# Node stages of a graph kernel: products in groups of four blocks, batch statistics, normalising block by block on ScalarE

## The reference, cut to what matters

```python
h = jnp.maximum(_layernorm(x, axis=-1), 0.0)
x = x + _L0_gnn_ref(h, ...)   # h @ W_w + W_b, attention by edge, weighted segment sum
h = jnp.maximum(_layernorm(x, axis=-1), 0.0)
x = x + _L1_gnn_ref(h, ...)   # a second layer norm inside; edge network; silu(x + agg) @ theta_w + theta_b
h = jnp.maximum(_layernorm(x, axis=-1), 0.0)
x = x + _L2_gnn_ref(h, ...)   # out = relu(x @ Wl + bl + mean_of_neighbours @ Wr + br); out / norm
h = jnp.maximum(_layernorm(x, axis=-1), 0.0)
x = x + _L3_gnn_ref(h, ...)   # h @ W.T, four attention heads, softmax by destination
```

## Time and profile before

| | us |
|---|---|
| median of three runs | 14312.43 (14309.55 to 14322.54) |
| profiled execution, span from first to last instruction | 14155.8 |
| what the runs' median has beyond this span | 156.6 |
| busy: TensorE / VectorE / ScalarE / GpSimd | 6866.6 / 6687.7 / 1674.0 / 7418.7 |

### The profile page before, as it was taken

One profiled execution on the slowest core, in us unless ns is written; L12 is line 12 of the kernel. 1 busy time (PEld: TensorE's weight loads), 2 busy tenths in 40 slices (PEclk: granted clock), 3 DMA queues, 4 the chain that ended last, 5 costly groups with the idle time before them and its releaser, 6 DMA issues. The chain is left out here.

```text
span 14155.8 us, 143364 instructions
## 1 busy us (share of the span) xinstructions
PE 6866.6 (49%) x36068; PEld 6019.9 (43%) x36069; DVE 6687.7 (47%) x23089; ACT 1674.0 (12%) x3503; POOL 7418.7 (52%) x7813
## 2 busy tenths in 40 slices
PE   1013333333344437777777523333233577777776
PEld 0013333333344325555555422222222476767775
DVE  4962222222477775555555432222224455555555
ACT  0001111111222211111111100000000100000000
POOL 0016666666555536666666346666662355555553
PEclk9996666666666668888888755555555555555555
DMA  0214443444333324444444511111113222323225
GB/s 17 105 46 127 128 129 124 129 128 127 115 92 87 91 73 121 120 123 121 121 124 120 109 40 47 47 47 47 47 47 28 58 81 81 81 81 81 81 80 80
DMA packets 1209149, 1249.60 MB, mean 88 GB/s; under 512 B 265607, under 2 KB 992220, under 8 KB 1208880
## 3 DMA queue, kind: packets, MB, share of 16 engines
q0 software_dynamic: 248832, 577.29, 16.5%
q1 hardware_dynamic: 957020, 668.72, 16.4%
q10 hardware_dynamic: 3156, 2.29, 0.0%
HBM read 842.78 MB, written 404.91 MB: 88 GB/s over the span
## 5 line engine op out<-in xcount | busy, mean ns | idle before, releaser
L920 POOL DMA_INDIRECT buf<-node_rows,buf x3456 | 3315.1, 959 | 2330.2 <-issue 1662.0
L1362 POOL DMA_INDIRECT buf<-node_rows_ln,buf x1728 | 1720.8, 996 | 1097.0 <-DVE buf L1491 614.8
L616 POOL DMA_INDIRECT edge_rows_by_src<-buf x1728 | 1686.0, 976 | 1069.3 <-ACT buf L626 547.6
L934 PE MATMUL psum<-buf 128*128 128x129 f32 x3456 | 768.5, 368 | 1796.6 <-issue 1335.2
L663 PE MATMUL psum<-buf 128*128 x3456 | 713.9, 373 | 1712.4 <-ACT buf L635 1155.2
L934 PEld LDWEIGHTS psum<-buf 128*128 128x128 f32 x3456 | 675.9, 276 | 1889.2 <-issue 1503.0
L663 PEld LDWEIGHTS psum<-buf 128*128 128x128 f32 x3456 | 644.7, 278 | 1769.0 <-issue 1768.1
L2024 PE MATMUL psum<-buf 128*128 128x132 f32 x3456 | 874.4, 412 | 576.3 <-issue 567.8
L944 DVE TENSOR_TENSOR agg<-agg,psum 128x129 f32 x864 | 250.4, 290 | 1868.4 <-remote 1609.3
L2024 PEld LDWEIGHTS psum<-buf 128*128 128x128 f32 x3456 | 772.6, 312 | 657.4 <-issue 656.0
L1014 POOL TENSOR_SCALAR buf<-buf 128x128 f32<-128x128 f32 x880 | 690.7, 800 | 665.0 <-PE psum L1064 623.8
(11 more groups left out here) (325 smaller groups left out, 12253.8 us busy)
## 6 DMA issues: line engine op xcount, KB each, us to landing
buf<-edge_rows_by_src SPq DMA_DIRECT2D x114, 1056.0 KB, 7.5
buf<-edge_rows_by_src SPq DMA_DIRECT2D x110, 1024.0 KB
buf<-in_edge_attr SPq DMA_DIRECT2D x864, 128.0 KB
running_weighted_sums<-buf SPq DMA_DIRECT2D x108, 544.0 KB
buf<-loc_rows_by_src SPq DMA_DIRECT2D x110, 512.0 KB
buf<-loc_rows_by_dst SPq DMA_DIRECT2D x110, 512.0 KB
running_sums<-buf SPq DMA_DIRECT2D x108, 512.0 KB
buf<-node_rows,buf POOLq DMA_INDIRECT x3456
```

Source lines behind the costliest of these rows:

```text
L616: nc.gpsimd.indirect_dma_start(rows, bass.IndirectOffsetOnAxis(ap=at[:, h, t:t + 1], axis=0), st[:, h, t, :], None).then_inc(scattered[h], 16)
L920: nc.gpsimd.indirect_dma_start(rows[:, t, 0:used], None, table, bass.IndirectOffsetOnAxis(ap=stage[:, t:t + 1], axis=0)).then_inc(sem, 16)
L934: last = nc.tensor.matmul(ps[:, q // 3, (q % 3) * W:(q % 3) * W + width], oh[:, 2 * q + s, :], rows[:, 2 * q + s, 0:width], start=(s == 0) ...
L1362: nc.gpsimd.indirect_dma_start(xn[:, j, t, :], None, table1, bass.IndirectOffsetOnAxis(ap=stage[:, j // 4, at:at + 1], axis=0)).then_inc(g ...
```

## The change

The helpers of the product are replaced. `GROUPS` are twelve groups of four blocks and one of a single block. `product_tensor` and `product_vector` are unrolled over the groups; `psT`, `hT` and `psO` exist twice and hold four blocks each; TensorE turns group g and then multiplies group g - 1, and VectorE copies group g and then takes out group g - 1. `ln_stats` becomes one batch-statistics instruction for each block and a short combination (`stats_done`). Normalising goes block by block to ScalarE in an activation with scale and offset by partition, also in `l1_nodes` and `l2_nodes`, where VectorE did it. `l1_nodes` splits every later step by groups, and ScalarE's location copies stand behind its second normalising. In `l1_finish` the bias is added before the wait for the sums. In `l2_nodes` the store is cut into four. In `l2_finish` ScalarE's copies are gone, since TensorE reads the table directly; the multiplication by the degree is cut into groups and stands behind the wait for the weights. `l3_nodes` changes as `l0_nodes` does. The edge stages are not touched.

The diff, cut: of the removed lines most are left out, since they stand in the functions printed above.

```diff
+GB = 4
+GROUPS = [(first, min(GB, NB - first)) for first in range(0, NB, GB)]
...
+        self.n = 0
+def stats_of_block(nc, st, b, block):
+    return nc.vector.bn_stats(st.parts[:, b, :], block)
+def stats_done(nc, dve, ch, st):
+    part = lambda k: st.parts[:, :, k:k + 1].rearrange("p b o -> p (b o)")
+    ch.link(nc.vector.tensor_tensor(st.gap[:], part(1), part(4), ALU.subtract))
+    nc.vector.tensor_tensor(st.mean[:], part(1), part(4), ALU.add)
+    ch.link(nc.vector.tensor_tensor(st.var[:], part(2), part(5), ALU.add))
+    ch.link(nc.vector.scalar_tensor_tensor(st.gap[:], st.gap[:], 0.25, st.gap[:], ALU.mult, ALU.mult))
+    ch.link(nc.vector.scalar_tensor_tensor(st.var[:], st.var[:], 1.0 / D, st.gap[:], ALU.mult, ALU.add))
+    nc.vector.tensor_scalar(st.var[:], st.var[:], LN_EPS, None, ALU.add).then_inc(st.var_ready, 1)
+    st.n += 1
+    dve.wait_ge(st.sd_ready, st.n)
+    ch.link(nc.vector.reciprocal(st.rstd[:], st.sd[:]))
+    ch.link(nc.vector.scalar_tensor_tensor(st.nmr[:], st.mean[:], -0.5, st.rstd[:], ALU.mult, ALU.mult))
...
+class NodeProduct:
+    def __init__(self, es, nc, sb, sem, terms):
+        self.terms = terms
+        self.hT = sb([P, 2, terms, GB * P])
+        self.psT = es.enter_context(nc.psum_tensor(fresh("psum"), [P, 2, terms, 512], F32))
+        self.psO = es.enter_context(nc.psum_tensor(fresh("psum"), [P, 2, 512], F32))
+        self.transposed, self.turned, self.produced, self.consumed = (sem() for _ in range(4))
+def product_tensor(nc, pe, m, ident, ready, blocks, weights):
+    for g in range(len(GROUPS) + 1):
+        if g < len(GROUPS):
+            first, count = GROUPS[g]
+            ready(g)
+            if g >= 2:
+                pe.wait_ge(m.turned, g - 1)
+            for k in range(m.terms):
+                for t in range(count):
+                    last = nc.tensor.transpose(m.psT[:, g % 2, k, t * P:(t + 1) * P], blocks(k, g, first + t, t), ident[:])
+            last.then_inc(m.transposed, 1)
+        if g:
+            count, b = GROUPS[g - 1][1], (g - 1) % 2
+            pe.wait_ge(m.turned, g)
+            if g >= 3:
+                pe.wait_ge(m.consumed, g - 2)
+            for t in range(count):
+                for k in range(m.terms):
+                    last = nc.tensor.matmul(m.psO[:, b, t * P:(t + 1) * P], m.hT[:, b, k, t * P:(t + 1) * P], weights[k], start=(k == 0), stop=(k == m.terms - 1))
+            last.then_inc(m.produced, 1)
+def product_vector(nc, dve, m, use):
+    for g in range(len(GROUPS) + 1):
+        if g < len(GROUPS):
+            count = GROUPS[g][1]
+            dve.wait_ge(m.transposed, g + 1)
+            if g >= 2:
+                dve.wait_ge(m.produced, g - 1)
+            nc.vector.tensor_copy(m.hT[:, g % 2, :, 0:count * P], m.psT[:, g % 2, :, 0:count * P]).then_inc(m.turned, 1)
+        if g:
+            first, count = GROUPS[g - 1]
+            dve.wait_ge(m.produced, g)
+            use(g - 1, first, count, m.psO[:, (g - 1) % 2, 0:count * P].rearrange("p (b d) -> p b d", d=D)).then_inc(m.consumed, 1)
...
 def l0_nodes(nc, c, ins, a_src):
...
+                for g, (first, count) in enumerate(GROUPS):
+                    if g >= 2:
+                        act.wait_ge(m.transposed, g - 1)
+                    for t in range(count):
+                        b = first + t
+                        last = nc.scalar.activation(h[:, g % 2, t, :], c["x"][:, b, :], ACT.Relu, bias=st.nmr[:, b:b + 1], scale=st.rstd[:, b:b + 1])
...
+                product_tensor(nc, pe, m, c["ident"], lambda g: pe.wait_ge(staged, g + 1), lambda k, g, b, t: h[:, g % 2, t, :], [w[:]])
...
+                for b in range(NB - 1):
+                    stats_of_block(nc, st, b, c["x"][:, b, :])
+                ch.link(stats_of_block(nc, st, NB - 1, c["x"][:, NB - 1, :]))
+                stats_done(nc, dve, ch, st)
                 dve.sem_inc(stats, 1)
-                ch.link(nc.vector.memset(tab[:], 0.0))
+                nc.vector.memset(tab[:, :, D:W], 0.0)
...
+                product_vector(nc, dve, m, lambda g, first, count, ps: nc.vector.tensor_tensor(
+                    tab[:, first:first + count, 0:D], ps, bc(wb[:].unsqueeze(1), [P, count, D]), ALU.add))
...
 def l1_nodes(nc, c, ins, blk_rows, table1, tab3, keep, loc_by_src):
...
             def _(act):
+                ln_sqrt(nc, act, own, 1)
+                act.wait_ge(own_done, 1)
+                for first, count in GROUPS:
+                    for b in range(first, first + count):
+                        last = nc.scalar.activation(f[:, b, :], c["x"][:, b, :], ACT.Relu, bias=own.nmr[:, b:b + 1], scale=own.rstd[:, b:b + 1])
+                    last.then_inc(rectified, 1)
+                ln_sqrt(nc, act, again, 1)
+                act.wait_ge(again_done, 1)
+                for first, count in GROUPS:
+                    for b in range(first, first + count):
+                        last = nc.scalar.activation(f[:, b, :], f[:, b, :], ACT.Identity, bias=again.nmr[:, b:b + 1], scale=again.rstd[:, b:b + 1])
+                    last.then_inc(normed, 1)
                 for g in range(QC):
                     act.wait_ge(loc_turned, g + 1)
                     nc.scalar.copy(loc_row[:, g].rearrange("p s k -> p (s k)"), psL[:, g % 2, 0:2 * P]).then_inc(loc_kept, 1)
+                for first, count in GROUPS:
+                    act.wait_ge(tabled, first // GB + 1)
+                    nc.scalar.copy(tab3[:, first:first + count, 0, :], f[:, first:first + count]).then_inc(high, 1)
+                for first, count in GROUPS:
+                    act.wait_ge(low_left, first // GB + 1)
+                    nc.scalar.copy(tab3[:, first:first + count, 1, :], tmp[:, first:first + count]).then_inc(middle, 1)
             @block.vector
             def _(dve):
                 ch = Chain(dve, dve_chain)
+                for b in range(NB - 1):
+                    stats_of_block(nc, own, b, c["x"][:, b, :])
+                ch.link(stats_of_block(nc, own, NB - 1, c["x"][:, NB - 1, :]))
+                stats_done(nc, dve, ch, own)
+                dve.sem_inc(own_done, 1)
                 dve.wait_ge(blocks_in, 16)
                 nc.vector.memset(keep[:, 0:1], 0.0)
                 nc.vector.tensor_tensor(keep[:, 1:NPX], pair_blk[:, 1:NPX], pair_blk[:, 0:NPX - 1], ALU.is_equal)
+                for g, (first, count) in enumerate(GROUPS):
+                    dve.wait_ge(rectified, g + 1)
+                    for b in range(first, first + count):
+                        last = stats_of_block(nc, again, b, f[:, b, :])
+                ch.link(last)
+                stats_done(nc, dve, ch, again)
+                dve.sem_inc(again_done, 1)
+                dve.wait_ge(loaded, 32)
+                for g, (first, count) in enumerate(GROUPS):
+                    part = f[:, first:first + count]
+                    dve.wait_ge(normed, g + 1)
+                    ch.link(nc.vector.tensor_tensor(part, part, bc(gb[:, 0:1], [P, count, D]), ALU.mult))
+                    nc.vector.tensor_tensor(part, part, bc(gb[:, 1:2], [P, count, D]), ALU.add).then_inc(tabled, 1)
+                for g, (first, count) in enumerate(GROUPS):
+                    dve.wait_ge(high, g + 1)
+                    nc.vector.tensor_tensor(tmp[:, first:first + count], f[:, first:first + count], tab3[:, first:first + count, 0, :], ALU.subtract).then_inc(low_left, 1)
+                for g, (first, count) in enumerate(GROUPS):
+                    dve.wait_ge(middle, g + 1)
+                    nc.vector.tensor_tensor(tab3[:, first:first + count, 2, :], tmp[:, first:first + count], tab3[:, first:first + count, 1, :], ALU.subtract)
...
 def l1_finish(nc, c, ins, table1, running, last_pairs):
...
+                for g, (first, count) in enumerate(GROUPS):
+                    act.wait_ge(summed, g + 1)
+                    if g >= 2:
+                        act.wait_ge(m.transposed, g - 1)
+                    nc.scalar.activation(h[:, g % 2, 0:count, :], tab[:, first:first + count, 0:D], ACT.Silu).then_inc(staged, 1)
...
+                dve.wait_ge(biased, 16)
+                nc.vector.tensor_tensor(x[:], x[:], bc(b[:].unsqueeze(1), [P, NB, D]), ALU.add).then_inc(based, 1)
+                dve.wait_ge(loaded, 32 + 16 * NB)
+                for first, count in GROUPS:
+                    nc.vector.tensor_tensor(tab[:, first:first + count, 0:D], tab[:, first:first + count, 0:D], agg[:, first:first + count, 0:D], ALU.add).then_inc(summed, 1)
+                dve.wait_ge(based, 1)
+                product_vector(nc, dve, m, lambda g, first, count, ps: nc.vector.tensor_tensor(
+                    x[:, first:first + count, :], x[:, first:first + count, :], ps, ALU.add))
...
 def l2_nodes(nc, c):
...
+                sp.wait_ge(filled, 1)
+                for first in range(0, NB, KB * 2):
+                    end = min(first + KB * 2, NB)
+                    sp.wait_ge(rectified, end)
```

(63 more changed lines are left out.)

122 lines of the change are left out of this document (28 added, 94 removed).

## The result

The changed kernel takes 13954.23 us (median of four runs, 13937.38 to 13969.52) against 14316.62 (four runs, 14309.55 to 14322.54): ratio 0.9743, interval 0.9731 to 0.9755. The forecast was 13980, in a range of 13935 to 14065.

What follows compares the result with a forecast made beforehand. Six node stages, each alone between barriers, were held bound by whole-tensor statistics chains and block-by-block hand-overs. Savings of 70.4, 47, 59, 22, 69 and 64.6 us made 332, taken from 14312.4: 13980 us, range 13935 to 14065.

Steps and rivals of the forecast that it cites:

- The base: Whole kernel: 156.6 us around the 14155.8 us profiled span stay as they are; savings come off the median 14312.43 us.
- Batch statistics: Statistics of the node stages: 0.26 us per instruction (0.20 to 0.43), 14.9 us a set, 13.4 us saved each time.
- Rival 2: Statistics: each batch-statistics instruction costs 0.43 us, giving 14015 us in total; chance 0.10.
- ScalarE's normalising: Node stages: one normalising instruction every 0.386 us, 18.9 us for 49 blocks; lower end 0.25 us.
- The clock: Product stages: TensorE slow for some 5 us, then at 2.4 GHz, a pass falling from 0.215 to 0.107 us.
- rival 1: Product stages: TensorE's clock stays at 1.2 GHz, so only 270 us are saved, 14042 us in total; chance 0.22.
- Product stages: First node stage, l1_finish, l2_finish and last node stage: 24, 30, 43 and 24 us from first feed to last use.
- l1_nodes: This stage: 77.5 us from its start to the last subtraction instead of 125.0, saving 47 us.
- l2_nodes: This stage: 38 us instead of 60.1, saving 22 us, with the last of four stores ending it.
- l2_finish: This stage: saves 69 us, with VectorE idle 3 to 4 us at the start, waiting for the weight loads.
- Rival 3: Product stages: engines don't overlap across groups, 4.3 us a group, 131 us less saved, 14111 us in total; chance 0.05.
- Rival 4: Edge stages: POOL-paced gathers get slower; at 0.08 us more per gather the total is 14395 us; chance 0.03.

## Why the prediction was right, and its terms

The sum was right in its mechanism and 20 us short (332 against 352.0); the total, 13980 against 13954.23, is 0.2% off. Every stage beat its forecast, so no stage's error hid another's; the batch-statistics price is the term that was mis-sized most.

- **The base.** The prediction took the span as 156.6 us short of a timed run for a constant reason. The reason was wrong (above), the step right, and here that was luck: it subtracted from the timed median. Subtracted from the profiled execution's time, the same 332 would have given about 13827.
- **Batch statistics.** Forecast pitch 0.26, bounds 0.20 to 0.43. Measured: (9.57 - 0.28)/48 = 0.194 us, the cheap row's price. A set ends 3.2 us earlier than forecast (12.1 where 14.9 and a hand-over of 0.4 stood); on the path four times, 12.8 of the missing 20 us. Rival 2 is out. The row to go by was that of the 0.20 us instruction; the per-element time of the old reductions misled.
- **ScalarE's normalising** was 0.386 forecast and measured: 18.95 us for 49.
- **The clock** rose 4 to 5 us into the products of every product stage, as forecast from the earlier trace rows; rival 1 (14042 us) is out. The Trainium skill's "TensorE: Matmul & The Clock Gate", Part 4 (PE-mode transpose), has it that the higher clock does not engage for transposes; this case's trace disagrees: 56 transposes with no product among them raised it from 0.50 to 1.00. That a third of transposes would keep the products slow too was the prediction's own step, and did not come about either.
- **Product stages**, 24, 30, 43 and 24 us forecast: 23.0, 8062.27 - 8034.93 = 27.3, 10658.27 - 10615.59 = 42.7 and 22.5. The 0.69 us is the length of one VectorE instruction; with nothing to wait for, the next starts 0.61 later (thirteen adds in 7.51 us; from PSUM too, 45.56 to 46.17 in the single-bank rows). That is 1.4 us in l1_finish's adds and 2.0 in l1_nodes' two subtractions. It also moves l1_finish's limit: not VectorE at 1.5 a group but TensorE, with a group every 8052.19 - 8050.85 = 1.34 us and busy for 3.00 of the 3.00 us from 8049.10 on.
- **l1_nodes**: 72.5 us from the start to the last subtraction, forecast 77.5. Of these 5.0 us, 3.2 are the first set and 2.0 the subtractions.
- **l2_nodes**: 8098.62 - 8062.58 = 36.0 us, forecast 38. The statistics gave 3.2, and the last store took some back: the next stage starts 8098.62 - 8093.63 = 5.0 us behind ScalarE's last block, where 3.8 stood.
- **l2_finish**: VectorE's gap for the weights was 3.86 us (forecast 3 to 4), and nothing else came up there.
- **Rival 3** (14111 us) is the single-bank run in kind; the change as written keeps the slowest engine of each stage at work.
- **Rival 4.** The edge stages after were 152 us longer than in the trace of before, which is that rival's picture and one of the prediction's own signs of being wrong. Repeated, they were 3 us shorter, so the change doesn't cause it; the two first traces alone could not have told. What makes an edge stage quick or slow in an execution stays open; more idle time before the gathers and on TensorE was seen. The chip of the first set of runs is not on record, so a difference between chips isn't excluded.

## What to carry to other kernels

A loop that hands one block at a time from engine to engine through single buffers costs the round trip of all its steps for every block, 1.49 us here, where the slowest engine alone needs 0.386. Give each hand-over a second buffer and write the order so that one block is turned while another is multiplied (0.53 here, unrolled, with TensorE at its higher clock), and make groups after that (0.386). Hold a whole-tensor chain against one instruction per block where the per-block form does more at once. Price an instruction in a run by the distance of starts, not by its length. Before a saving is subtracted, compare the profiled execution with the timed runs, and if they disagree, take the timed ones and expect the unchanged stages to differ between traces.

## What was not expected of the hardware

- The same kernel takes 14316.62 us in one set of runs and 12126.16 in another, while each repeats itself within 0.2%; all but 2 us of it is between the node stages, where the gathers are.
- With one bank and gaps, the same loop got the faster passes at very different times: 9.5 us after TensorE's first pass in the first stage (28.87 to 38.39), 32 us after it in the last one (9369.23 to 9401.18). Until then its records fill about 2.8 of every 3.74 us, from then on about 1.7 of every 2.67, and it does not fall back within the stage. What decides stays open.
- The wide products of the earlier trace rows ran in the trace of after for 12.28 us without a gap (from 10773.11) and at 0.50 all the way. So busy time alone, as the records count it, doesn't tell when the clock rises here; why these passes stay slow is open.
- 56 transposes with no product among them raised the granted clock from 0.50 to 1.00.
- In the first node stage the granted-clock column doesn't agree with the passes: in its first groups eight passes take 1.92 us, as they do at 0.50 elsewhere, while the column shows 1.00. There the pass length is the surer reading.
